# The products for keys, rotated queries and folded queries of a latent attention: two full-precision matmuls each, or five or six on rounded high and low parts

## The chip, the cores and the metric

The program runs on one core of a Trainium2 chip. The metric is the device time of one execution in microseconds; before the change it is the median of three executions. All values that enter and leave are float32.

## The reference, cut to what matters

Two transformer layers on 1024 tokens of 256 values. Only the first layer's attention is touched, and of it the part that makes rotated keys, rotated queries and folded queries:

```python
q_mid = rmsnorm(h @ q_a_w.T, q_a_ln_w)                 # 1024 x 192
q = (q_mid @ q_b_w.T)                                  # 16 heads of 128 + 64
q_nope, q_pe = q[..., :128], q[..., 128:]
kv_lora, k_pe = kv_a[..., :64], kv_a[..., 64:]         # kv_a = h @ kv_a_w.T, k_pe: 16 heads of 64
kv = rmsnorm(kv_lora, kv_a_ln_w) @ kv_b_w.T            # k_nope and v of each head
q_pe, k_pe = apply_rope(q_pe, cos, sin), apply_rope(k_pe, cos, sin)
scores = einsum(concat(q_nope, q_pe), concat(k_nope, k_pe)) * scale
probs = softmax(scores)
main_out = (probs @ v) @ o_w.T
# beside it a "pattern" attention with 16 heads of 16, then gates that mix the two,
# a mixture of experts, and a second layer
```

The kernel never forms `k_nope`: for each head `q_nope @ k_nope.T` is computed as (q_mid times a folded 192 x 64 matrix) times the 64 normalised values `kvT` that all heads share.

## The kernel before, in words

All orders are written out by hand: `pattern_order()`, `main_order()` and others list steps, and each of the five engines (TensorE, VectorE, ScalarE, GpSimd, and SP, which issues the DMAs) walks the same lists and executes its own part of each step; semaphores join them. Every engine's queue is in order.

The stages that matter here are these. Up to about 100 us the first layer's normalisation, the pattern attention's projections (`stgr`, through DRAM into `qstr`, `kstr`), the latents and the fold run. `act_latents` writes `qmTa` (q_mid transposed, values 0 to 127) and `qmTb` (values 128 to 191 in rows 0 to 63), and `act_fold` writes the folded matrices `waba` and `wabb`. From then to about 293 us comes the pattern attention: score matmuls (L1414), exponentials (L1435), value matmuls (L1457) and, running ahead, the maxima: max matmuls (L1281), reductions on VectorE (L1289), and the casts of the maxima (L1302, L1304), which the shift matmuls (L1314) need. From 306 to about 810 us comes the main attention in 32 units of 256 queries by 2 heads; four units are a pair of heads with all queries. A unit has four scores (L1712 to L1714, each on rounded high and low parts, on tiles `qk0h`, `qk0l`, `qk1h`, `qk1l`), a maximum on VectorE (L1721), exponentials (L1736), eight groups of four transposes (L1745) each with a copy (L1758 on ScalarE, L1763 on VectorE), one batch of value matmuls (L1805) and an output projection (L1826).

The products fill `qk0*` and `qk1*`. There are six for each pair p of heads, in the order of `FIRST`: R0 and R1 (rotated keys, two halves of the tokens), R2 (rotated queries, first half), Q0 and Q1 (folded queries), R3 (rotated queries, second half). Each is 128 x 512 and needs two matmuls over a contraction of 256 (keys) or 192 padded to 256 (queries), at L1536 in `pe_part`. Pair 0's six lie in the pattern attention, every eighth step, each cut in two around a max matmul (`pe_first`); pair p+1's lie in the first of pair p's units, one behind every fifth group of transposes (`PREP_EVERY`, `pe_prep`). Behind a product ScalarE copies the bank to `t12` (L1574); for a rotated one SP swaps its 32-row blocks with four DMAs (L1584), and GpSimd multiplies by cosines (L1596) and sines (L1598, which needs the swap), adds (L1601), and casts and subtracts into high and low parts (L1615, L1622); a folded one needs only the last two. `pe_score` waits, before the first score of each half pair, for the high and low parts that it reads. Three banks (4, 5, 7) turn round among transposes, projections and products, and each waits for its copy.

SP's queue holds, besides the swaps, the DMAs that write a unit's shares of the softmax to DRAM (`sp_shares`) and read them back spread over rows (`sp_spread`).

Of the kernel before, what the change touches and what calls it, by code (L numbers as in the profile page):

```python
# [334 lines left out]
def program(nc, a, out):  # L335
# [30 lines left out]
    x = sb("x", [128, NT, D], F32)  # L366
    hT = sb("hT", [128, 2, T], F32)
# [2762 lines left out]
```

## Time and profile before

| | |
|---|---|
| median of three executions | 1343.31 us (1342.86 to 1344.18) |
| profiled execution, its own time | 1348.52 us |
| its span, first to last instruction | 1346.6 us, mean granted TensorE clock 0.972 |
| busy share of TensorE, VectorE, ScalarE, GpSimd | 95%, 58%, 55%, 36% |
| line L1536 | 192 records of TensorE, 592 to 594 ns median as modelled |

A matmul's modelled duration overlaps the next one's, so what a matmul takes of the stream is read from start to start or from the chain, not from its own duration. A full-precision float32 matmul leaves two records (with one weight load each), a rounded one leaves one. An idle time in brackets stands ahead of the instruction, with what ended it.

### The profile page before, as it was taken

How to read it: one execution, taken by the hardware profiler on the slowest of the kernel's cores; microseconds unless marked ns; L12 is line 12 of the kernel's file. 1: busy time of each engine (PE TensorE's matmuls, PEld its weight loads, DVE VectorE, ACT ScalarE, POOL GpSimd, SP SyncE). 2: the span in 40 equal slices, each digit the busy share in tenths (PEclk: the TensorE clock that was granted, in tenths of full speed). 3: DMA queues.
4: the chain of work that ended last, by engine and by line, in shares of the span. 5: the costliest groups of instructions: out<-in, count | busy, mean ns of one | idle time of the engine just before them, and what ended most of it. 6: DMA issues, size and time to landing. Idle time of an engine off the chain costs nothing.

```text
span 1346.6 us, 22054 instructions
## 1 busy us (share of the span) xinstructions
PE 1278.6 (95%) x8233; PEld 873.7 (65%) x8233; DVE 776.1 (58%) x1221; ACT 734.5 (55%) x1364; POOL 487.3 (36%) x439
## 2 busy tenths in 40 slices
PE   7879999999999999999999999999978998889998
PEld 5633443357777777777777777788853444578997
DVE  4478987624545444444444566654767774575555
ACT  3438987775555555555555554333245667435553
POOL 5260045224656657474655303445200000331221
PEclk9969999999999999999999999999999999899999
DMA  8734000001010111111111203001331510101110
GB/s 330 192 75 82 1 10 17 9 1 29 20 33 17 31 25 24 25 24 24 24 24 25 63 13 138 24 25 47 72 81 39 114 36 1 32 15 32 49 40 32
DMA packets 54866, 63.90 MB, mean 47 GB/s; under 512 B 23997, under 2 KB 41149, under 8 KB 53693
## 3 DMA queue, kind: packets, MB, share of 16 engines
q1 hardware_dynamic: 54760, 62.50, 17.4%
q8 instruction: 66, 1.08, 0.4%
q14 instruction: 40, 0.32, 0.1%
HBM read 45.64 MB, written 8.45 MB: 40 GB/s over the span
## 4 chain that ended last, share of the span: by engine, by line
PE 82%; DVE 10%; ACT 3%; issue 2%; DMA 2%; SPq 0%; POOL 0%; ACTq 0%; DVEq 0%; POOLq 0%
PE bank L1805 9%; PE bank L1745 8%; PE bank L1457 7%; PE bank L1536 6%; PE bank L2002 5%; PE bank L2004 5%; PE bank L2003 5%; PE bank L1712 4%; PE bank L1714 4%; PE bank L1713 4%; PE bank L1414 4%; PE bank L1281 2%; PE bank L1826 2%; DVE mpc L1356 2%; PE bank L1394 2%
## 5 line engine op out<-in xcount | busy, mean ns | idle before, releaser
L1721 DVE TENSOR_REDUCE nmq<-bank 128x1 f32<-128x1024 f32 x128 | 156.5, 1223 | 163.8 <-PE bank L1714 163.7
L1435 ACT ACTIVATE Pb<-bank 128x512 f32<-128x512 f32 (+3 forms) x355 | 180.8, 573 | 36.6 <-PE bank L1414 14.1
L1758 ACT ACTIVATE Pt<-bank 128x512 f32<-128x512 f32 x187 | 110.6, 594 | 121.9 <-PE bank L1745 121.0
L1289 DVE TENSOR_REDUCE mp<-bank 128x2 f32<-128x1024 f32 x128 | 154.2, 1223 | 34.0 <-PE bank L1281 33.2
L1736 ACT ACTIVATE Pq<-bank,nmq 128x1024 f32<-128x1024 f32 x127 | 141.7, 1115 | 56.3 <-DVE nmq L1721 56.2
L1745 PE MATMUL bank<-idf,Pq 128*128 128x128 f32 x1016 | 145.8, 275 | 1.4 <-ACT Pq7l L1736 1.2
L1745 PEld LDWEIGHTS bank<-idf,Pq 128*128 128x128 f32 x1016 | 119.2, 140 | 39.3 <-issue 15.6
L1712 PE MATMUL bank<-qk1h,qk0h 128*128 128x512 f32 x256 | 120.6, 471 | 0.0
L1356 DVE TENSOR_REDUCE mpc<-bank 128x2 f32<-128x1024 f32 (+2 forms) x96 | 88.4, 954 | 47.5 <-PE bank L1344 25.2
L1805 PE MATMUL bank<-Pt,kvx 128*64 128x256 f32 x992 | 114.1, 382 | 0.0
L1457 PE MATMUL bank<-Pb,vx 128*17 128x256 f32 (+3 forms) x1222 | 108.9, 416 | 0.7 <-ACT OTa L1471 0.5
L1714 PE MATMUL bank<-qk1h,qk0l 128*128 128x512 f32 x256 | 101.2, 395 | 0.0
L1713 PE MATMUL bank<-qk1l,qk0h 128*128 128x512 f32 x256 | 100.4, 392 | 0.0
L1805 PEld LDWEIGHTS bank<-Pt,kvx 128*64 128x64 f32 x992 | 68.6, 137 | 40.5 <-issue 9.3
L1598 POOL TENSOR_TENSOR t<-t,sinT 128x512 f32<-128x512 f32 x32 | 41.0, 1280 | 107.0 <-DMA t<-t 107.0
L1977 POOL TENSOR_TENSOR cTt<-cTt,gab 128x256 f32<-128x256 f32 x8 | 6.1, 758 | 190.6 <-DVE cTt L1972 190.4
L1414 PE MATMUL bank<-qstr,kstr 64*128 64x512 f32 x256 | 72.1, 507 | 1.0 <-ACT Pb L1435 0.6
L2204 POOL TENSOR_TENSOR hl<-hf,hh 128x512 fp32r<-128x512 f32 x32 | 41.2, 1288 | 84.1 <-ACT hh L2191 84.1
L1596 POOL TENSOR_TENSOR Rt<-t,cosT 128x512 f32<-128x512 f32 x32 | 41.0, 1282 | 72.9 <-ACT t L1574 71.0
L2416 POOL TENSOR_TENSOR v1l<-wr,v1h 128x512 fp32r<-128x512 f32 x25 | 32.1, 1289 | 96.3 <-ACT v1h L2411 96.3
L1414 PEld LDWEIGHTS bank<-qstr,kstr 64*128 64x128 f32 x256 | 28.6, 188 | 58.2 <-ACT Pb L1435 36.4
L1816 DVE TENSOR_TENSOR OTm<-bank,Rs 128x256 f32<-128x256 f32 x32 | 13.6, 424 | 89.4 <-PE bank L1805 87.1
(344 smaller groups left out, 2948.5 us busy)
## 6 DMA issues: line engine op xcount, KB each, us to landing
t<-t SPq DMA_DIRECT2D x128, 64.0 KB
wr<-wf SPq DMA_DIRECT2D x25, 256.0 KB, 2.7
wraw<-wf SPq DMA_DIRECT2D x8, 768.0 KB, 4.3
scratch<-stgr SPq DMA_DIRECT2D x4, 1024.0 KB, 7.8
Rs<-shares SPq DMA_DIRECT2D x64, 64.0 KB, 3.8
scratch<-stg SPq DMA_DIRECT2D x8, 384.0 KB, 2.6
qst<-scratch SPq DMA_DIRECT2D x9, 256.0 KB, 8.6
owT<-owT SPq DMA_DIRECT2D x1, 2048.0 KB, 11.3
```

The costliest lines, as they stand in the source:

```text
L1289: e.tensor_reduce(mp[:, w % 3, :, j, kh], wide[slot][:], AX, ALU.max).then_inc(ring_ok, 1)
L1356: e.tensor_reduce(mpc[:, w // 2 % 3, a0:a0 + 2, j, kh], wide[slot][:, :, 0:c], AX, ALU.max).then_inc(ring_ok, 1)
L1414: e.matmul(bank[b][:], kst2[r, hp, kt * 128:kt * 128 + 128], qst2[r, hp, cols(half)], start=True, stop=True).then_inc(st_mm[0], 1)
L1435: e.activation(PBR[l][i % len(PBR[l])][:, 0:c], bank[b][:, 0:c], ACT.Exp, scale=0.25).then_inc(exp_ok[0], 1)
L1457: last = e.matmul(bank[6][32 * a:32 * a + 17, to:to + c], vx[:, t, h * 17:h * 17 + 17], PBR[l][i % len(PBR[l])][:, q0:q0 + c], start=(t == ...
L1712: e.matmul(o, qh[:, qs], kh[:, ks], start=True, stop=False)
L1713: e.matmul(o, qh[:, qs], kl[:, ks], start=False, stop=False)
L1714: last = e.matmul(o, ql[:, qs], kh[:, ks], start=False, stop=True)
L1721: e.tensor_reduce(nmq[:, n % 8:n % 8 + 1], scores(u, i), AX, ALU.max, negate=True).then_inc(mp_ok, 1)
L1736: e.activation(probabilities(u, i)[:], scores(u, i), ACT.Exp, bias=nmq[:, n % 8:n % 8 + 1], accum_out=sums[:, u % 2, i:i + 1]).then_inc(ex ...
L1745: last = e.transpose(bank[b][:, 128 * c:128 * c + 128], probabilities(u, 2 * (c % 2) + c // 2)[:, 128 * k:128 * k + 128], idf[:])
L1805: last = e.matmul(bank[6][64 * hd:64 * hd + 64, 0:256], kvx[:, k, :], transposed(u, k)[:, 256 * hd:256 * hd + 256], start=(k < 1), stop=(k ...
```

## The change

Operands of the six products are no longer read as float32. Each is split into a rounded part ("high", type fp32r) and the rounded remainder ("low"), and a product becomes the sum of high x high, low x high and high x low. Six rounded matmuls make a key product, five a query product.

- Moving operands, once, on GpSimd in `pool_rounded`, behind its pattern memsets and ahead of pair 0: `hT` gives `kmh` and `kml` (`kml` lies over `hT`), `qmTa` gives `qah` and `qal`. Of the 64 values in `qmTb` SP first makes a second copy in rows 64 to 127 (`sp_below`, two DMAs with the one for the folded matrices); `qbs` then holds the high part in rows 0 to 63 and the low part in rows 64 to 127, so that its stationary operand, with the weights in both halves of the rows, makes high x high and low x high in one matmul.
- Weights: `wkpe`, `wqpa`, `wqpb`, which were loaded whole, are loaded pair by pair, 128 KB each, into `wks` and `wqs`, and GpSimd splits them into `wkh`, `wkl`, `wqh`, `wql`; it splits the folded ones, `wab`, into `lth`, `ltl`. The load of the next keys' weights is issued behind R2's swap, that of the queries' behind R0's swap; the splits stand behind Q0 (keys), R3 (folded) and R0 (queries).
- GpSimd's two memsets at the start (`pool_rest`) go.

```diff
 
         cs = cols(ROPE[part[1]][1] if part[0] == "rope" else part[1])
         if part[0] == "rope" and ROPE[part[1]][0] == 1:
-            two = [(wkpe[:, k, p, :], hT[:, k, cs]) for k in range(2)]
-        elif part[0] == "rope":
-            two = [(wqpa[:, p, :], qmTa[:, cs]), (wqpb[:, p, :], qmTb[:, cs])]
+            if 0 in ks:
+                e.wait_ge(wt_ok, SPLIT2["k", p])
+                e.wait_ge(rounded, 12)
+            two = [[(wkh[:, k, :], kmh[:, k, cs]), (wkh[:, k, :], kml[:, k, cs]), (wkl[:, k, :], kmh[:, k, cs])] for k in range(2)]
         else:
-            two = [(w[:, 2 * p:2 * p + 2, :].rearrange("p h c -> p (h c)"), q[:, cs]) for w, q in ((waba, qmTa), (wabb, qmTb))]
+            if part[0] == "rope":
+                hi, lo = wqh, wql
+                if 0 in ks:
+                    e.wait_ge(wt_ok, SPLIT2["q", p])
+            else:
+                hi, lo = lth, ltl[:, :, p, :]
+                if 0 in ks:
+                    e.wait_ge(wt_ok, SPLIT2["lat", p])
+            if 0 in ks:
+                e.wait_ge(rounded, ROUNDED)
+            two = [[(hi[:, 0, :], qah[:, cs]), (hi[:, 0, :], qal[:, cs]), (lo[:, 0, :], qah[:, cs])],
+                   [(hi[:, 1, :], qbs[:, cs]), (lo[:, 1, :], qbs[:, cs])]]
         for k in ks:
-            last = e.matmul(o, *two[k], start=(k == 0), stop=(k == 1))
+            for n, (w, q) in enumerate(two[k]):
+                last = e.matmul(o, w, q, start=(k == 0 and n == 0), stop=(k == 1 and n == len(two[1]) - 1))
         if 1 in ks:
             last.then_inc(rp_mm if part[0] == "rope" else lt_mm, 1)
 
@@ -1543,11 +1578,6 @@
         b, free = BANK_P0[k]
         if not second:
             e.wait_ge(*free)
-            if k == 0:
-                e.wait_ge(d_w4, 48)
-                e.wait_ge(lat_ok, LAT_ALL)
-                e.wait_ge(fold_ok, 6)
-                e.wait_ge(rest_ok, 2)
         pe_part(e, 0, FIRST[k], bank[b][:], (1,) if second else (0,))
...
-    def pool_rest(e):
-
-        e.memset(qmTb[64:128, :], 0.0).then_inc(rest_ok, 1)
-        e.memset(wabb[64:128, :, :], 0.0).then_inc(rest_ok, 1)
-        e.wait_ge(rest_ok, 2)
+    def sp_below(e):
+
+        e.wait_ge(lat_ok, LAT_ALL)
+        e.dma_start(qmTb[64:128, :], qmTb[0:64, :]).then_inc(d_below, 16)
+        e.wait_ge(fold_ok, 6)
+        e.dma_start(wab[64:128, 1, :, :], wab[0:64, 1, :, :]).then_inc(d_below, 16)
+
+    def pool_rounded(e):
+
+        e.wait_ge(pj_mm, 8)
+        e.wait_ge(gate_mm, 4)
+        e.wait_ge(gate_v, 8)
+        for k, h in itertools.product(range(2), range(2)):
+            e.tensor_copy(kmh[:, k, cols(h)], hT[:, k, cols(h)]).then_inc(rounded, 1)
+        for k, q in itertools.product(range(2), range(4)):
+            ts = slice(256 * q, 256 * q + 256)
+            e.wait_ge(rounded, 2 * k + q // 2 + 1)
+            e.tensor_tensor(kml[:, k, ts], hT[:, k, ts], kmh[:, k, ts].bitcast(F32), ALU.subtract).then_inc(rounded, 1)
+        e.wait_ge(lat_ok, LAT_ALL)
+        for h in range(2):
+            e.tensor_copy(qah[:, cols(h)], qmTa[:, cols(h)]).then_inc(rounded, 1)
+        for q in range(4):
+            ts = slice(256 * q, 256 * q + 256)
+            e.wait_ge(rounded, 12 + q // 2 + 1)
+            e.tensor_tensor(qal[:, ts], qmTa[:, ts], qah[:, ts].bitcast(F32), ALU.subtract).then_inc(rounded, 1)
+        e.wait_ge(d_below, 32)
+        for h in range(2):
+            e.tensor_copy(qbh[:, cols(h)], qmTb[:, cols(h)]).then_inc(rounded, 1)
+        e.wait_ge(rounded, 20)
+        for q in range(4):
+            ts = slice(256 * q, 256 * q + 256)
+            e.tensor_tensor(qbs[64:128, ts], qmTb[64:128, ts], qbh[64:128, ts].bitcast(F32), ALU.subtract).then_inc(rounded, 1)
+        e.wait_ge(rounded, 24)
+        for h in range(2):
+            e.tensor_copy(qbs[0:64, cols(h)], qmTb[0:64, cols(h)]).then_inc(rounded, 1)
+        e.wait_ge(rounded, ROUNDED)
+
+    def sp_weights_k(e, p):
+
+        if p:
+            e.wait_ge(rp_mm, 4 * p - 2)
+        e.dma_start(wks[:], a["wkpe"][p]).then_inc(d_wk, 16)
+
+    def sp_weights_q(e, p):
+
+        if p:
+            e.wait_ge(rp_mm, 4 * p)
+        e.dma_start(wqs[:], a["wqpe"][p]).then_inc(d_wq, 16)
+
+    def pool_weights_k(e, p):
+        e.wait_ge(d_wk, 16 * (p + 1))
+        if p:
+            e.wait_ge(rp_mm, 4 * p - 2)
+        e.tensor_copy(wkh[:], wks[:]).then_inc(wt_hi, 1)
+        e.wait_ge(wt_hi, SPLIT2["k", p])
+        e.tensor_tensor(wkl[:], wks[:], wkh[:].bitcast(F32), ALU.subtract).then_inc(wt_ok, 1)
+        e.wait_ge(wt_ok, SPLIT2["k", p])
+
+    def pool_weights_q(e, p):
+        e.wait_ge(d_wq, 16 * (p + 1))
+        if p:
+            e.wait_ge(rp_mm, 4 * p)
+        e.tensor_copy(wqh[:], wqs[:]).then_inc(wt_hi, 1)
+        e.wait_ge(wt_hi, SPLIT2["q", p])
+        e.tensor_tensor(wql[:], wqs[:], wqh[:].bitcast(F32), ALU.subtract).then_inc(wt_ok, 1)
+        e.wait_ge(wt_ok, SPLIT2["q", p])
+
+    def pool_weights_l(e, p):
+        if p:
+            e.wait_ge(lt_mm, 2 * p)
+        else:
+            e.wait_ge(fold_ok, 6)
+            e.wait_ge(d_below, 32)
+        e.tensor_copy(lth[:], wab[:, :, 2 * p:2 * p + 2, :].rearrange("p a h c -> p a (h c)")).then_inc(wt_hi, 1)
+        e.wait_ge(wt_hi, SPLIT2["lat", p])
+        e.tensor_tensor(ltl[:, :, p, :], wab[:, :, 2 * p:2 * p + 2, :].rearrange("p a h c -> p a (h c)"), lth[:].bitcast(F32), ALU.subtract).then_inc(wt_ok, 1)
+        e.wait_ge(wt_ok, SPLIT2["lat", p])
...
         pool_stack2(e, slice(4, 8))
+        pool_rounded(e)
+        pool_weights_k(e, 0)
+        pool_weights_q(e, 0)
+        pool_weights_l(e, 0)
         for p in range(8):
             if p < 2:
                 pool_keys(e, p)
             for k in range(len(FIRST)):
                 pool_product(e, p, k)
+                if k == 0 and p:
+                    pool_weights_q(e, p)
+                elif k == 3 and p < 7:
+                    pool_weights_k(e, p + 1)
+                elif k == 5 and p < 7:
+                    pool_weights_l(e, p + 1)
         for s in MAIN:
...
-        for d, n in ((wkpe, "wkpe"), (wqpa, "wqpa"), (wqpb, "wqpb")):
-            e.dma_start(d[:], a[n]).then_inc(d_w4, 16)
+        sp_weights_k(e, 0)
+        sp_weights_q(e, 0)
         sp_scratch2(e, 2)
         sp_scratch2(e, 3)
         sp_stack2(e, 2)
         e.dma_start(cosT[:], a["cosT"]).then_inc(d_cs, 16)
         e.dma_start(sinT[:], a["sinT"]).then_inc(d_cs, 16)
+        sp_below(e)
         for k in range(len(FIRST)):
             sp_swap(e, 0, k)
+            if k == 2:
+                sp_weights_k(e, 1)
         for s in MAIN:
             if s[0] == "prep":
                 sp_swap(e, s[1], s[2])
+                if s[2] == 0:
+                    sp_weights_q(e, s[1])
+                elif s[2] == 2 and s[1] < 7:
+                    sp_weights_k(e, s[1] + 1)
```

In the host's layout `wkpe` and `wqpe` become pair-major, and `wqpe`'s second half repeats the 64 rows.

On TensorE, R2 of pair 1, behind four transposes in unit 1. The names are the moving operand and then the stationary one. Before:

```order
L1745 MATMUL bank<-idf,Pq_155 128x128
L1745 MATMUL bank<-idf,Pq_159 128x128
L1536 MATMUL bank<-qmTa,wqpa 128x512
L1536 MATMUL bank<-qmTb,wqpb 128x512
L1712 MATMUL bank<-qk1h_131,qk0h_129 128x512
```

and of the change:

```order
L1847 MATMUL bank<-idf,Pq_163 128x128
L1847 MATMUL bank<-idf,Pq_167 128x128
L1571 MATMUL bank<-qah,wqh 128x512
L1571 MATMUL bank<-qal,wqh 128x512
L1571 MATMUL bank<-qah,wql 128x512
L1571 MATMUL bank<-qbs,wqh 128x512
L1571 MATMUL bank<-qbs,wql 128x512
L1814 MATMUL bank<-qk1h_139,qk0h_137 128x512
```

Two matmuls became five at the same place, between the same transposes and the same score.

On GpSimd, the end of R0 of pair 1 and the start of R1. Before:

```order
L1615 CAST qk1h_136<-Rt 64x512
L1622 TENSOR_TENSOR qk1l_143<-Rt,qk1h_135 64x512
L1622 TENSOR_TENSOR qk1l_144<-Rt,qk1h_136 64x512
L1596 TENSOR_TENSOR Rt<-t_145,cosT 128x512
L1598 TENSOR_TENSOR t_145<-t_145,sinT 128x512
```

and of the change:

```order
L1645 CAST qk1h_144<-Rt 64x512
L1652 TENSOR_TENSOR qk1l_151<-Rt,qk1h_143 64x512
L1652 TENSOR_TENSOR qk1l_152<-Rt,qk1h_144 64x512
L1718 CAST wqh<-wqs 128x256
L1720 TENSOR_TENSOR wql<-wqs,wqh 128x256
L1626 TENSOR_TENSOR Rt<-t_153,cosT 128x512
L1628 TENSOR_TENSOR t_153<-t_153,sinT 128x512
```

The split of the query weights stands between the two products.

On SP, from the last table to the first DMA of unit 0's spread (20 swap DMAs are five products'). Before:

```order
L2951 DMA cosT<-cosT 128x1024
L2952 DMA sinT<-sinT 128x1024
L1584 DMA t_145<-t_145 32x512 x20
L1781 DMA shares<-rcp_60 128x4x1
L1792 DMA Rs<-shares 64x2x128 x2
```

and of the change:

```order
L3062 DMA cosT<-cosT 128x1024
L3063 DMA sinT<-sinT 128x1024
L1659 DMA qmTb<-qmTb 64x1024
L1661 DMA wab<-wab 64x1024
L1614 DMA t_153<-t_153 32x512 x12
L1697 DMA wks<-wkpe 128x256
L1614 DMA t_153<-t_153 32x512 x8
L1703 DMA wqs<-wqpe 128x256
L1883 DMA shares<-rcp_60 128x4x1
L1894 DMA Rs<-shares 64x2x128 x2
```

The two copies stand behind the tables, a load of key weights behind the third swap, and a load of query weights between a swap and the shares.

## Rows read from the trace of the kernel before

**Rows 1.** The page: busy us, share of the span, instructions.
```profile
PE 1278.6 (95%) x8233; PEld 873.7 (65%) x8233; DVE 776.1 (58%) x1221; ACT 734.5 (55%) x1364; POOL 487.3 (36%) x439
```

**Rows 2.** Busy time by windows: the first of the main stage's.
```profile
core 0: us, PE busy (x) PEld busy (x) DVE busy (x) ACT busy (x) POOL busy (x), PEclk, DMA share, GB/s
...
306.00:365.00 59.00, 59.00 (x344) 42.88 (x343) 28.89 (x37) 32.80 (x58) 32.59 (x31) 1.00 0.12 26
```

**Rows 3.** The chain that ended last, 320 to 420 us.
```profile
by line: PE bank L1745 22.7%; PE bank L1805 21.6%; PE bank L1536 15.6%; PE bank L1714 11.9%; PE bank L1712 11.6%; PE bank L1713 11.5%; PE bank L1826 5.2%
...
326.48 1.72 PE bank L1536 x4
```

**Rows 4.** The same chain, 730 to 860 us: start, length, what.
```profile
731.10 3.60 PE bank L1805 x32
...
748.28 3.60 PE bank L1805 x32
...
762.06 3.60 PE bank L1805 x32
```

**Rows 5.** Line L1536: ns min, median, max of its key matmuls.
```profile
L1536 PE MATMUL bank<-hT,wkpe x64: 592/592/697, 187.3 to 708.8; 128*128 128x512 f32 x64
```

**Rows 6.** Timeline of TensorE, 440 to 475 us: start, duration.
```profile
448.14 1.04 PE L1745 MATMUL bank<-idf,Pq 128*128 128x128 f32 x8
...
449.48 0.39 PE L1714 MATMUL bank<-qk1h,qk0l 128*128 128x512 f32 x1
449.71 0.39 PE L1712 MATMUL bank<-qk1h,qk0h 128*128 128x512 f32 x1
...
450.40 0.60 PE L1745 MATMUL bank<-idf,Pq 128*128 128x128 f32 x4
```

**Rows 7.** The chain that ended last, 184 to 306 us.
```profile
187.33 1.08 PE bank L1536 x2
...
188.84 1.05 PE bank L1536 x2
...
269.04 0.51 ACT Pb L1435
```

**Rows 8.** Timeline of GpSimd, 0 to 260 us.
```profile
33.44 1.59 POOL L1056 TENSOR_TENSOR raw<-raw,lnw 128x256 f32<-128x256 f32 x2 [2.79 <-ACT raw L1008]
...
186.27 2.13 POOL L1640 CAST qk1h<-kvT 64x1024 fp32r<-64x1024 f32 x2 [85.84 <-issue]
...
197.45 1.29 POOL L1615 CAST qk1h<-Rt 64x512 fp32r<-64x512 f32 x2
198.83 2.64 POOL L1622 TENSOR_TENSOR qk1l<-Rt,qk1h 64x512 fp32r<-64x512 f32 x2
```

**Rows 9.** DMA issues: KB each, median us from issue to landing.
```profile
cosT<-cosT SPq DMA_DIRECT2D x1, 512.0 KB, 17.4
```

**Rows 10.** Timeline of all engines, 96 to 113 us.
```profile
96.92 3.51 POOL L906 MEMSET kstr<- 16x4096 f32 x1
...
98.47 2.00 DVE L1302 CAST mc<-nm 128x8 fp32r<-128x8 f32 x1
...
112.52 0.17 DVE L1302 CAST mc<-nm 128x8 fp32r<-128x8 f32 x1
```

**Rows 11.** Timeline of all engines, 320 to 353 us, pair 1.
```profile
323.01 1.27 POOL L1596 TENSOR_TENSOR Rt<-t,cosT 128x512 f32<-128x512 f32 x1 [0.17 <-POOL qk1l L1622]
...
345.59 2.61 POOL L1622 TENSOR_TENSOR qk0l<-t,qk0h 64x512 fp32r<-64x512 f32 x2
...
350.97 0.48 PE L1712 MATMUL bank<-qk1h,qk0h 128*128 128x512 f32 x1
```

**Rows 12.** Timeline of all engines, 501 to 523 us, pair 4.
```profile
501.53 2.46 SPq L1584 DMA_DIRECT2D t<-t  x4
...
505.50 1.27 POOL L1598 TENSOR_TENSOR t<-t,sinT 128x512 f32<-128x512 f32 x1 [2.40 <-DMA t<-t]
...
509.64 2.63 POOL L1622 TENSOR_TENSOR qk1l<-Rt,qk1h 64x512 fp32r<-64x512 f32 x2
...
522.10 1.02 PE L1536 MATMUL bank<-qmTa,wqpa 128*128 128x512 f32 x2
```

More of the change, by code:

```diff
@@ L405, in program @@
     WKPE = A.at
-    wkpe = A.sb("wkpe", [128, 2, 8, 128], F32)
+    kmh = A.sb("kmh", [128, 2, T], F32R)
     WQP = A.at
-    wqpa = A.sb("wqpa", [128, 8, 128], F32)
-    wqpb = A.sb("wqpb", [128, 8, 128], F32)
+    qah = A.sb("qah", [128, T], F32R)
+    WQS = A.at
+    wqs = A.sb("wqs", [128, 2, 128], F32)
+    wqh = A.sb("wqh", [128, 2, 128], F32R)
+    wkh = A.sb("wkh", [128, 2, 128], F32R)
+    lth = A.sb("lth", [128, 2, 128], F32R)
     WAB = A.at
-    waba = A.sb("waba", [128, 16, 64], F32)
-    wabb = A.sb("wabb", [128, 16, 64], F32)
+    wab = A.sb("wab", [128, 2, 16, 64], F32)
     MO = A.at
@@ L427, in program @@
     gsb = A.sb("gsb", [128, 2], F32)
+    kml = sb("kml", [128, 2, T], F32R, at=HT)
+    qal = sb("qal", [128, T], F32R, at=QMT)
+    qbs = sb("qbs", [128, T], F32R, at=QMT + 4 * T)
+    qbh = sb("qbh", [128, T], F32R, at=WSP)
+    wql = sb("wql", [128, 2, 128], F32R, at=WQS)
+    ltl = sb("ltl", [128, 2, 8, 128], F32R, at=WAB)
     pctx = sb("pctx", [128, NT, D], F32, at=HTP)
@@ L980, in pool_vx_ones @@
         e.memset(vx[:].rearrange("p i (h c) -> p (i h) c", c=17)[:, :, 16:17], 1.0).then_inc(vx_one, 1)
-    d_w2, d_k, d_w3, d_w4, d_cs = sem("d_w2"), sem("d_k"), [sem("d_w30"), sem("d_w31")], sem("d_w4"), sem("d_cs")
+    d_w2, d_k, d_w3, d_cs = sem("d_w2"), sem("d_k"), [sem("d_w30"), sem("d_w31")], sem("d_cs")
     raw_mm, raw_ok, gw_ok = sem("raw_mm"), sem("raw_ok"), sem("gw_ok")
     rms_v, rms_s, gat_v, gat_s = sem("rms_v"), sem("rms_s"), sem("gat_v"), sem("gat_s")
-    qkv_ok, kvx_ok, lat_mm, lat_ok, lnw_ok = (sem(n) for n in (
-        "qkv_ok", "kvx_ok", "lat_mm", "lat_ok", "lnw_ok"))
+    qkv_ok, lat_mm, lat_ok, lnw_ok = (sem(n) for n in (
+        "qkv_ok", "lat_mm", "lat_ok", "lnw_ok"))
     LAT_ALL = 6
@@ L1087, in act_latents @@
         e.activation(kvT[:, cs], bank[6][:], ACT.Copy).then_inc(lat_ok, 1)
-    rest_ok = sem("rest_ok")
+    d_wk, d_wq, d_below = sem("d_wk"), sem("d_wq"), sem("d_below")
+    rounded, wt_hi, wt_ok = sem("rounded"), sem("wt_hi"), sem("wt_ok")
+    ROUNDED = 26
+    SPLITS = [("k", 0), ("q", 0), ("lat", 0)]
+    for p_ in range(1, 8):
+        SPLITS += [("k", p_), ("lat", p_), ("q", p_)]
+    SPLIT2 = {s_: n_ + 1 for n_, s_ in enumerate(SPLITS)}
     fold_mm, fold_ok, fold_v = sem("fold_mm"), sem("fold_ok"), sem("fold_v")
     def fold_rows(g):
-        return (128, waba, 8 * (g // 2), 0) if g % 2 == 0 else (64, wabb, 8 * (g // 2), 128)
+        return (128, wab[:, 0, :, :], 8 * (g // 2), 0) if g % 2 == 0 else (64, wab[:, 1, :, :], 8 * (g // 2), 128)
     def fold_bank(g):
@@ L3066, in layout @@
     kpe = kva[64:].reshape(8, 2, 64, 256)[:, ::-1].reshape(1024, 256).T
-    d["wkpe"] = np.ascontiguousarray(kpe.reshape(2, 128, 8, 128).transpose(1, 0, 2, 3))
+    d["wkpe"] = np.ascontiguousarray(kpe.reshape(2, 128, 8, 128).transpose(2, 1, 0, 3))
     qb = i["L0_attn_q_b_w"].reshape(16, 192, 192)
     qpe = qb[:, 128:, :].reshape(8, 2, 64, 192)[:, ::-1].reshape(8, 128, 192).transpose(2, 0, 1)
-    d["wqpa"], d["wqpb"] = np.ascontiguousarray(qpe[:128]), cat(qpe[128:], np.zeros_like(qpe[128:]))
+    d["wqpe"] = np.ascontiguousarray(np.stack([qpe[:128], cat(qpe[128:], qpe[128:])], 1).transpose(2, 0, 1, 3))
     d["qbn"] = np.ascontiguousarray(qb[:, :128, :].transpose(1, 0, 2))
```

6 lines of the change are left out of this document (4 added, 2 removed).

## The prediction

> **What bounds the kernel now.** I read the page first: TensorE is busy 95% of the span [rows 1], which alone says little, since ends of matmuls are modelled. So next the windows of 59 us over the stage where 42 of the 48 changed products run, units 0 to 27 of the main attention, from 306 us: in the first TensorE is busy for all 59 us at a granted clock of 1.00 (the 2.4 GHz level), VectorE, ScalarE and GpSimd for 29 to 33 [rows 2]; the seven behind it read alike. Then the chain that ended last, in 100 us of that stage: TensorE's lines make up all of it, with no wait for another engine and no issue time, and L1536, the changed line, is 15.6% [rows 3]. Last, a test of whether a shorter product shortens the stream: the same batch (L1805) starts 17.18 us apart where two products lie between and 13.78 apart where none does, so (17.18 - 13.78) / 2 = 1.70 us for one [rows 4]. The chain itself has 1.72 for a product [rows 3]. So without products the stream runs on with nothing else taking the room: a microsecond off L1536 is one off the span, until something else is late.
>
> **The products.** A product is two full-precision matmuls of 512 columns, each two records (64 records for the 32 key matmuls [rows 5]; the other 64 matmuls are the same shape). Four records are 1.72 us, 0.43 each. The change issues six rounded matmuls for a key product (two halves of the contraction, each high x high, low x high, high x low) and five for a rotated or folded query one (three and two, since the second half carries high and low parts in one operand). Their price stands in the score matmuls: the same shape on rounded operands, each with its own stationary operand as here. Transposes end at 448.14 + 0.87 = 449.01 (0.87 is two groups at the chain's 0.44), the next start at 450.40, six matmuls between: 1.39 / 6 = 0.232 us; start to start two rows have 0.23 [rows 6]. A key product becomes 6 x 0.232 = 1.39 and saves 0.33; another becomes 5 x 0.232 = 1.16 and saves 0.56. Seven pairs in the main stage: 7 x (2 x 0.33 + 4 x 0.56) = 20.3 us.
>
> A page speaks to this. The Trainium skill, "FP8 and Floating Point Precision", TensorE Precision Notes, says that true FP32 takes four passes through the array. Two such matmuls would be eight passes against six or five, 0.215 us a pass, and 27.5 us saved over 48 products, if all passes cost alike. The rows agree on 0.43 for a record of two passes but have 0.232 for a rounded matmul.
>
> **The first pair** has its six products in the pattern attention, each cut in two around two max matmuls, 1.08 + 1.05 us on the chain [rows 7]. The surplus of 0.4 over 1.72 I put down to the switches between full-array and 64-row matmuls, which stay; the rest changes as above, 2 x 0.33 + 4 x 0.56 = 2.9 us. Behind them the chain crosses an exponential of ScalarE here and there [rows 7], so 0 is the other end; I take 2.9, since most steps there are TensorE's. So far 23.2 us.
>
> **GpSimd's one-time rounding.** GpSimd is idle for 85.84 us up to 186.27. A cast of 512 columns takes 1.29 / 2 = 0.64, a subtraction of 512 takes 2.64 / 2 = 1.32, one of 256 half of that [rows 8]. Keys: four casts and eight quarters, 2.6 + 5.3; queries: six casts and eight quarters, 3.9 + 5.3; together 17 us, and under 4 for three weight splits. In between it waits for two transfers that copy rows 0 to 63 to rows 64 to 127, which stand behind the cosine tables on SP's queue; the tables took 17.4 us to land [rows 9], the copies would land near 118. Ready near 130, against the first product at 187.33: the idle time hides it, uncovered it would cost its 20 us.
>
> What it can cost there is VectorE's casts of the maxima (L1302). One that met a GpSimd memset took 2.00 us and ended as the memset did; the next, with GpSimd idle, took 0.17 [rows 10]. Two casts, near 112 and 123, now meet GpSimd instructions of 0.32 to 0.66 us. Bounds 0 and 1.3 us; I take 0.2, since only the rest of an instruction is waited for and one cast in two leads the chain at all. The Trainium skill, "GPSIMD Engine Reference", Specifications, says that GpSimd shares its SBUF interfaces with VectorE; the trace agrees with its 2.00 against 0.17.
>
> **Weight splits in the loop.** Three times a pair GpSimd gains a cast and a subtraction of 128x256: 0.32, and 0.66 to 0.80 (two multiplications of that shape take 1.59 [rows 8]), with hand-overs 1.1 to 1.3 us. That is 3.3 to 3.9 us in a pair of 4 x 13.78 + 6 x 1.70 = 65.3 us, of which GpSimd is busy 36 [rows 2]. Its queue is in order, so what stands behind a split matters:
> - The query split stands behind R0. In pair 1, R1 starts 0.17 us after R0's last subtraction, so there is no slack, and R1, R2 and Q0 shift by 1.1 to 1.3. Q0's low part, which the first score of unit 4 needs, ended at 345.59 + 2.61 = 348.20, and that score started at 350.97, 2.8 us in hand [rows 11]. By then TensorE is 2 x 0.33 + 3 x 0.56 = 2.3 us earlier: a stall of 0.6 to 0.8, I take 0.8.
> - In pair 4, R0's GpSimd work ends at 509.64 + 2.63 = 512.27, and R2, the next product with query weights, starts at 522.10 [rows 12]: 9.8 us for a split of 1.3.
> - The key and folded splits stand behind Q0 and R3. Products come five transposes apart, some 10 us, and a folded one takes GpSimd 1.28 + 2.64, a rotated one some 12: the lag of one is made good by the next.
> - TensorE's new waits before a product are for semaphores reached before; the score at 350.97 has seven waits and no idle time ahead of it [rows 11]. Nothing.
>
> **SP's queue** loses three transfers of 2 MB near 44 us and gains two of 128 KB there, the two copies, and 14 of 128 KB in the loop, behind R0's and R2's swap. One costs some 2.46 / 4 = 0.6 us of issue [rows 12]; it delays what is queued behind it, the shares and through them R1's swap. That wait lies beside the shift above: nothing more, 1 us a pair as the other end. The two memsets removed from GpSimd's start had nobody waiting: nothing.
>
> **Sum:** 23.2 - 0.2 - 0.8 = 22.2 us off. The profiled execution, 1348.52, becomes 1326.3; it is 5.2 us above the median of the three runs, so I forecast 1343.31 - 22.2 = **1321.1**.
>
> **Rivals.**
> - *Some is swallowed* (0.12): the first pair's 2.9 go to ScalarE behind them, and the loop gives another microsecond back. 22.2 - 3.9 = 18.3, 1325. For: the exponential in the chain. Against: it is one of few.
> - *GpSimd, the swaps and ScalarE's copies fall behind in every pair* (0.17). For: R1 goes back to back behind R0 in pair 1, and a pair gets 3 us shorter while GpSimd's work grows by 3.9. Against: GpSimd is idle for 29 us of each pair, mostly in waits for later things. At 1 to 2 us in each of seven pairs, 7 to 14 back: 1328 to 1335.
> - *A rounded matmul costs a pass, 0.215* (0.04): 256 x 0.017 = 4.3 more off, 1316.8; so by the page above. Against: 0.23 in every score.
> - *Slower* (0.03). The query weights land late: their transfer is issued behind R0's swap, near 504, and R2 starts at 522.10 - 0.7. With a split of 1.3 the transfer may take 16 us; R0's swap landed 1.5 us after its last issue, by GpSimd's start at 505.50 [rows 12], but the cosine tables took 17.4. Each microsecond above 16 stalls TensorE, with every transpose and score behind it, in seven pairs; from 16 + 22.2 / 7 = 19.2 us it decides for slower, and 21 us gives 1343.3 + 7 x 1.8 = 1356.
> - *It does not do what it says* (0.02): rounded matmuls on these operands run as two records of 0.43. 256 x 0.86 = 220 against 48 x 1.72 = 83 us: 1480.
>
> **Numbers.** The forecast case, 1319 to 1324, has 0.62. The range 1317 to 1330 takes in the pass-pace case, the swallowed one and the cheap end of falling behind, and leaves some 0.17 out. 0.2% is 2.7 us, about what a measurement of this kernel can tell from no change: faster 0.93, same 0.02 (the dearest end of falling behind), slower 0.05.
>
> **What would show it.** Right: 256 single records on the product line, 0.23 apart; L1805's batches some 16.1 us apart with two products between and 13.78 with none; a chain of TensorE alone in the loop, but for a stall under 1 us before unit 4's first score; GpSimd's rounding over before 135 us. Wrong: TensorE waiting for low parts or weight splits in several pairs; ScalarE's copy of a product held by a swap with scores waiting behind it; VectorE casts of over a microsecond near 112 us; rounded products at another pace.

## The result, and the profile after

The changed kernel takes 1323.84 us, median of four executions (1316.35 to 1326.55), against 1343.74 for the kernel before beside it (1342.86 to 1344.27): a ratio of 0.9846, 95% interval 0.9824 to 0.9869, so 17.6 to 23.7 us off. In a later session five executions have a median of 1321.97, ratio 0.9853 (0.9829 to 0.9877). The profiled execution took 1326.55 us, its span 1324.6.

The page of the changed kernel: busy time, and the granted clock of TensorE in 40 slices of 33 us.

```profile
PE 1253.9 (95%) x8297; PEld 884.3 (67%) x8297; DVE 775.9 (59%) x1221; ACT 732.5 (55%) x1364; POOL 530.4 (40%) x511
...
PEclk9979999999999999999999999999979999899999
```

Beside [rows 1], TensorE's busy time is 25 us less and its share the same 95%: the share told nothing before and tells nothing now. GpSimd has 43 us more; VectorE and ScalarE have what they had, within 2 us. Where the time went is seen in the chain that ended last. The changed kernel, two stretches of it (start, length, what):

```profile
503.30 1.39 PE bank L1571 x6
...
512.81 0.59 PE bank L1847 x4
513.40 1.16 PE bank L1571 x5
...
712.19 3.60 PE bank L1907 x32
...
728.25 3.60 PE bank L1907 x32
741.99 3.60 PE bank L1907 x32
755.74 3.60 PE bank L1907 x32
```

L1571 is the product line, L1907 the batch of value matmuls. A key product is six records in 1.39 us, another five in 1.16, where four records took 1.72 [rows 3]. The batches stand 728.25 - 712.19 = 16.06 us apart with two products between them, and 13.75 with none; before it was 17.18 and 13.78 [rows 4].

What the whole change gave to the stage it is in is read between two marks: the start of the first product, and the start of the last addition of the main attention's output into x, on VectorE. First and last start stand in the rows of one line (count, ns min/median/max, then the starts). The kernel before, then the changed one in a second trace of it:

```profile
L1536 PE MATMUL bank<-hT,wkpe x64: 592/592/697, 187.3 to 708.8; 128*128 128x512 f32 x64
L1840 DVE TENSOR_TENSOR x<-x,bank x32: 677/689/691, 330.9 to 818.6; 128x512 f32<-128x512 f32 x32
```

```profile
L1571 PE MATMUL bank<-kmh,wkh x32: 389/474/500, 185.0 to 685.9; 128*128 128x512 f32 x32
L1942 DVE TENSOR_TENSOR x<-x,bank x32: 675/687/692, 324.9 to 793.8; 128x512 f32<-128x512 f32 x32
```

818.6 - 187.3 = 631.3 us before and 793.8 - 185.0 = 608.8 after: 22.5 less. I call this time "the stage" below, and "the loop" the units of the main attention in it. The first trace of the changed kernel has 613.0: it lost 4.2 us in one place, which the section on the prediction takes up.

### The profile page after: what moved, and what is told of

It is laid out like the page before. It is cut to its first block, busy times and chain, and to the rows that moved or that the text cites. A ratio compares the mean times of both kernels' runs of the same rounds, so it can differ in the third digit from the quotient of the medians.

```text
span 1324.6 us, 22340 instructions
## 1 busy us (share of the span) xinstructions
PE 1253.9 (95%) x8297; PEld 884.3 (67%) x8297; DVE 775.9 (59%) x1221; ACT 732.5 (55%) x1364; POOL 530.4 (40%) x511
## 4 chain that ended last, share of the span: by engine, by line
PE 77%; DVE 11%; DMA 4%; ACT 3%; issue 3%; SPq 2%; POOL 1%; ACTq 0%; DVEq 0%; POOLq 0%
PE bank L1907 8%; PE bank L1847 8%; PE bank L1479 7%; PE bank L2104 6%; PE bank L2105 6%; PE bank L2106 6%; PE bank L1571 4%; PE bank L1814 4%; PE bank L1436 4%; PE bank L1816 4%; PE bank L1815 4%; DVE mp L1311 2%; PE bank L1303 2%; PE bank L1928 2%; DVE mpc L1378 2%
## 5 line engine op out<-in xcount | busy, mean ns | idle before, releaser
L1838 ACT ACTIVATE Pq<-bank,nmq 128x1024 f32<-128x1024 f32 x127 | 141.6, 1115 | 52.2 <-DVE nmq L1823 52.1
L1907 PE MATMUL bank<-Pt,kvx 128*64 128x256 f32 x992 | 114.1, 382 | 0.0
L1814 PE MATMUL bank<-qk1h,qk0h 128*128 128x512 f32 x256 | 109.8, 429 | 0.0
L1816 PE MATMUL bank<-qk1h,qk0l 128*128 128x512 f32 x256 | 101.3, 396 | 0.0
L1907 PEld LDWEIGHTS bank<-Pt,kvx 128*64 128x64 f32 x992 | 68.6, 137 | 37.7 <-issue 6.6
L1628 POOL TENSOR_TENSOR t<-t,sinT 128x512 f32<-128x512 f32 x32 | 41.0, 1281 | 99.7 <-DMA t<-t 99.7
L1303 PE MATMUL bank<-kstr,qstr 64*128 64x512 f32 x256 | 59.9, 445 | 3.7 <-DVE mp L1311 3.6
```

The lines of the kernel that those rows point to most:

```text
L1814: e.matmul(o, qh[:, qs], kh[:, ks], start=True, stop=False)
L1816: last = e.matmul(o, ql[:, qs], kh[:, ks], start=False, stop=True)
L1838: e.activation(probabilities(u, i)[:], scores(u, i), ACT.Exp, bias=nmq[:, n % 8:n % 8 + 1], accum_out=sums[:, u % 2, i:i + 1]).then_inc(ex ...
L1907: last = e.matmul(bank[6][64 * hd:64 * hd + 64, 0:256], kvx[:, k, :], transposed(u, k)[:, 256 * hd:256 * hd + 256], start=(k < 1), stop=(k ...
```

## The experiments

Every kernel was traced. The table has, from the trace, the start of the first product, the stage, what lies behind it up to the end of the span, and TensorE's idle time from 304 to 366 us, the first of seven windows of 62 us (62 less its busy time). In the other six windows TensorE is busy for all 62 us in every kernel, but for 428 to 490 in the first trace. The ratio is to the executions of the kernel before in the same session.

| kernel | median us (executions) | ratio, 95% | first product | stage | behind | idle |
|---|---|---|---|---|---|---|
| before, two traces | 1343.74 (4), 1343.21 (1) | | 187.3, 184.1 | 631.3, 631.3 | 528.0, 525.9 | 0, 0 |
| changed, first trace | 1323.84 (4) | 0.9824 to 0.9869 | 185.6 | 613.0 | 526.0 | 0.59 |
| the same, second | 1321.97 (5) | 0.9829 to 0.9877 | 185.0 | 608.8 | 526.2 | 0.44 |
| the same, third | 1324.35 (1) | | 184.9 | 608.7 | 528.8 | 0.64 |
| no loads in the loop | 1320.81 (6) | 0.9815 to 0.9867 | 186.0 | 608.4 | 521.3 | 0.26 |
| no work on weights in the loop | 1323.40 (6) | 0.9830 to 0.9880 | 187.3 | 609.7 | 528.9 | 1.62 |
| longer splits | 1326.88 (4) | 0.9834 to 0.9898 | 185.5 | 609.8 | 530.5 | 1.70 |
| no swaps | 1325.27 (4) | 0.9821 to 0.9906 | 185.9 | 608.4 | 523.5 | 0 |
| swap in two DMAs | 1326.08 (4) | 0.9827 to 0.9900 | 188.3 | 613.3 | 524.3 | 3.58 |
| keys in fp32 | 1326.20 (6) | 0.9838 to 0.9896 | 186.2 | 614.1 | 526.0 | 0.88 |
| high parts only | 1292.55 (4) | 0.9590 to 0.9649 | 186.7 | 577.3 | 529.0 | 1.90 |
| the same, no low weights made | 1292.02 (4) | 0.9584 to 0.9662 | 185.8 | 575.4 | 527.2 | 2.33 |

Read the columns against each other. Ahead of the first product and behind the stage, where these kernels differ little or not at all, one trace and the next differ by up to 4 and 9 us, whatever the kernel; unedited kernels give 631.3 twice, and 608.8 and 608.7. So the stage shows 0.5 us where a median shows 3, unless a transfer is late as in the first trace (613.0).

**The changed kernel again, unedited.**

> The changed kernel once more, unedited, for its spread (1316.35 to 1326.55 us in four runs, where the kernel before has 1342.86 to 1344.27). Theory A (the weights' loads and splits inside the loop make GpSimd and the swaps late, now in one pair, now in another, and TensorE then stands and loses its clock): again a spread of some 10 us, median 1321 to 1325, and the profile shows one or two stops of 1 to 3 us in the loop at a rotation's swap or a low part. Theory B (the stop in pair 3 of the first profile was a single late landing that any run may have): median nearer 1318, and no stop in most pairs; the spread would then be there in the next two kernels too.

Neither theory's case as written. The median, 1321.97, is theory A's, but the one stop in the stage, at pair 1's products, is of 0.44 us where A wanted 1 to 3, and the spread was 1321.4 to 1325.55 and not 10 us; pair 3 has no stop, as theory B had it. And the premise fell: the kernel before, in the same session, went from 1338.76 to 1349.78 in eleven executions. The spread is in both kernels.

**No loads of weights in the loop.**

```diff
-            if k == 2:
-                sp_weights_k(e, 1)
...
-                if s[2] == 0:
-                    sp_weights_q(e, s[1])
-                elif s[2] == 2 and s[1] < 7:
-                    sp_weights_k(e, s[1] + 1)
```

> Leaves out the key and query weights' loads of pairs 1 to 7 (14 DMAs of 128 KB on SyncE's queue); the splits stay, each reading what the last one left. Theory A, in the form that the loads hold up the swaps behind them: 3 to 6 us under the unedited kernel of the same call (about 1318), spread under 2 us, no swap landing over 7 us. In the form that GpSimd's splits do it: same as unedited, within 1 us. Theory B (late landings are chance): same median within 1 us, spread of some 10 us stays.

On GpSimd (not shown) each split of pairs 1 to 7 reads what the last one left, so its work stays. The stage is 608.4 against 608.8 and 608.7, the spread still 9 us (1317.64 to 1326.97). The 14 loads cost at most 0.4 us altogether.

**No work on weights in the loop.**

```diff
-                if k == 0 and p:
-                    pool_weights_q(e, p)
-                elif k == 3 and p < 7:
-                    pool_weights_k(e, p + 1)
-                elif k == 5 and p < 7:
-                    pool_weights_l(e, p + 1)
...
-                e.wait_ge(wt_ok, SPLIT2["k", p])
+                e.wait_ge(wt_ok, SPLIT2["k", 0])
```

> Leaves out all work on weights inside the loop: the loads of pairs 1 to 7 and the splits of the key, query and folded weights; every pair multiplies with pair 0's rounded weights. TensorE does the same matmuls. Theory A: 1316 to 1318, spread under 2 us, the copy of Q1 in pair 1 no longer waits for the low parts of Q0. Theory B: the median falls by the 1.3 us of pair 1's wait at most, and the spread stays.

The stage is 609.7, no shorter than unedited, and the median 1323.40 where theory A wanted 1316 to 1318. ScalarE's copies of products to `t12` in pair 1, in the kernel without any work on weights (start, duration, idle time before it and its releaser):

```profile
336.06 0.60 ACT L1604 ACTIVATE t<-bank 128x512 f32<-128x512 f32 x1 [4.07 <-DMA t<-t]
...
346.91 0.60 ACT L1604 ACTIVATE t<-bank 128x512 f32<-128x512 f32 x1 [3.13 <-POOL qk0l L1652]
```

The second is Q1's copy, which waits for Q0's low part because both go through `t12`. It waits 3.13 us with the splits gone; unedited, it waits 1.96:

```profile
340.71 2.65 POOL L1652 TENSOR_TENSOR qk0l<-t,qk0h 64x512 fp32r<-64x512 f32 x2
...
343.45 0.60 ACT L1604 ACTIVATE t<-bank 128x512 f32<-128x512 f32 x1 [1.96 <-POOL qk0l L1652]
...
344.10 0.66 PE L1847 MATMUL bank<-idf,Pq 128*128 128x128 f32 x4 [0.44 <-ACT t L1604]
```

By itself this doesn't clear the splits, since R2's swap was slower in this execution. What does is the chain that ended last, traced back from the stop. Unedited:

```profile
309.10 8.17 DMA shares<-rcp
...
317.29 0.66 SPq L1894
...
318.71 0.56 SPq L1614
...
320.58 2.19 DMA t<-t
...
322.83 1.30 POOL t L1628
...
325.62 0.51 SPq L1614
...
327.44 5.00 DMA t<-t
...
332.51 1.29 POOL t L1628
```

A unit's shares go to DRAM (8.17 us). The DMAs that read them back (L1894) wait for that in SP's queue, and R1's swap (the first L1614) is issued behind them. R1's multiplication by the sines (L1628), R2's swap, R2's sines, Q0's low part and Q1's copy follow. No split of weights is in this chain, and no work on R0. It is the same chain without work on weights, with R2's swap slow in the issue itself:

```profile
327.80 3.48 SPq L1614
...
331.32 2.61 SPq L1614
...
333.97 1.98 DMA t<-t
...
336.02 1.29 POOL t L1628
```

Counted from the first product, in all traces whose TensorE does the same matmuls and whose swaps in pair 1 are complete and not late:

| kernel | R1's sines start | R2's sines start | idle |
|---|---|---|---|
| changed, three traces | 137.7, 137.8, 138.0 | 147.7, 147.5, 147.6 | 0.59, 0.44, 0.64 |
| no loads | 136.8 | 147.3 | 0.26 |
| no work on weights | 137.2 | 148.7 | 1.62 |
| longer splits (next run) | 137.7 | 148.8 | 1.70 |

The idle time is the start of R2's sines less 147.1, within 0.15 us in all six. That start is set by R2's swap, which took 6.9 to 7.7 us from its first issue to there in the first four traces, 8.8 without work on weights and 7.9 with longer splits; why it varies no run shows. R1's sines come 0.5 to 1.2 us earlier only where the loads are gone, which fits the load's issue ahead of the shares in SP's queue. So the 1.62 us is the slower swap and no price of this edit, and the splits are not what makes Q0's low part late.

That low part ends at 340.71 + 2.65 = 343.36 unedited. From the last addition behind the pattern attention (301.4, and 306.2 before) that is 142.0 us, and the 348.20 of before [rows 11] is 142.0 too (142.1 and 142.2 in the other traces of the changed kernel, 141.6 in the other of before). It hardly moved, while TensorE comes to Q1 2.3 us earlier (two key products and three others). Before, Q1's copy started at 348.55, 0.35 us behind that low part:

```profile
348.55 0.60 ACT L1574 ACTIVATE t<-bank 128x512 f32<-128x512 f32 x1 [0.51 <-PE bank L1536]
```

2.3 less 0.35 is close to the 1.96 us that ScalarE now waits, and TensorE, with transposes behind that copy, stands for the last 0.44 of it.

**Longer splits.** Each cast of weights is made four times.

```diff
-        e.tensor_copy(wqh[:], wqs[:]).then_inc(wt_hi, 1)
-        e.wait_ge(wt_hi, SPLIT2["q", p])
+        for n in range(4):
+            e.tensor_copy(wqh[:], wqs[:]).then_inc(wt_hi, 1)
+            e.wait_ge(wt_hi, 4 * SPLIT2["q", p] - 3 + n)
```

> Each split of weights has its cast four times in place of once, some 1.4 us more GpSimd work for each of three splits a pair, so the split takes 2.6 us and GpSimd is busy 45 of 62 us. Theory A (steady pairs have room, pair 1 alone is late): pairs 2 to 7 stay at 62.3 us and TensorE without idle time; pair 1 loses 1.4 us more for the query split ahead of Q0, 610 to 611.5 us from the first product to the last addition into x. Rival (GpSimd's lag passes from pair to pair, as the forecast's third case had it): each pair loses 1 to 4 us, 617 or more.

The stage is 609.8, 1.0 to 1.1 more than unedited, all of it in the first window (idle 1.70 against 0.44 to 0.64); six windows are full, with GpSimd busy 45 of 62 us in five of them. That looks like theory A's pair 1, but the table above says otherwise: R1's sines start where they did, and R1's sum at most 0.3 us later (139.45 us from the first product against 139.1 to 139.4). The rest is R2's swap, slower by 0.7 to 1.0 us. So a split longer by 1.4 us is free in six pairs of seven and costs at most 0.3 us in pair 1.

**No swaps.** GpSimd multiplies the unswapped copy by the sines, and ScalarE's next copy waits for that multiplication in place of the swap (not shown).

```diff
-        for q in range(4):
-            e.dma_start(t12[32 * (q ^ 1):32 * (q ^ 1) + 32, 1, :], t12[32 * q:32 * q + 32, 0, :]).then_inc(d_sw, 16)
...
-            e.wait_ge(d_sw, 64 * (r + 1))
-            e.tensor_tensor(t12[:, 1, :], t12[:, 1, :], sinT[:, cs], ALU.mult).then_inc(rp_sin, 1)
+            e.tensor_tensor(t12[:, 1, :], t12[:, 0, :], sinT[:, cs], ALU.mult).then_inc(rp_sin, 1)
```

> Leaves out the four DMAs of each rotation's swap (GpSimd multiplies the unswapped copy by sinT); all of GpSimd's instructions, the weights' loads and splits and TensorE's stay. Theory C (the one stop left in the loop, in pair 1, comes from TensorE now reaching pair 1's products some 4 us earlier while each product on GpSimd still waits 2 to 4 us for its swap; the weights have nothing to do with it, since without them the wait for Q0's low part was 3.1 us against 2.0): no idle time of TensorE between 304 and 366 us, 608.2 to 608.6 us from the first product to the last addition into x, and no wait of ScalarE's copies for GpSimd. Rival (GpSimd's own work in pair 1, rounding and splits, is the hold): the wait for the low part of Q0 stays at 1 us or more, idle time over 0.3 us.

Windows of the changed kernel unedited, of the one without work on weights and of the one without swaps, 304 to 366 us (length, then busy us of TensorE, its weight loads, VectorE, ScalarE, GpSimd; granted clock, DMA share, GB/s):

```profile
304.00:366.00 62.00, 61.56 (x391) 48.54 (x391) 32.28 (x43) 37.80 (x67) 41.49 (x43) 1.00 0.15 33
```

```profile
304.00:366.00 62.00, 60.38 (x379) 47.92 (x378) 30.43 (x41) 34.92 (x62) 36.51 (x35) 1.00 0.13 27
```

```profile
304.00:366.00 62.00, 62.00 (x391) 49.18 (x391) 33.06 (x43) 37.43 (x66) 42.92 (x44) 1.00 0.09 16
```

With 42.92 us of GpSimd's work and no swap there is no idle time; with 36.51 us of work and the swaps there is the most of the three. Theory C stands: the hold is in the swaps. The run takes away both parts of that hold at once, the transfers and R1's place behind the shares in SP's queue, so it doesn't say which counts for how much. The stage is 608.4.

**Swap in two DMAs.**

```diff
-        for q in range(4):
-            e.dma_start(t12[32 * (q ^ 1):32 * (q ^ 1) + 32, 1, :], t12[32 * q:32 * q + 32, 0, :]).then_inc(d_sw, 16)
+        for q in range(2):
+            e.dma_start(t12[64 * (q ^ 1):64 * (q ^ 1) + 64, 1, :], t12[64 * q:64 * q + 64, 0, :]).then_inc(d_sw, 16)
```

> Moves the same bytes of each swap in two DMAs of 64 partitions in place of four of 32 (halves of 64 rows change places, where the rotation wants halves of 32 within each head). SyncE issues for 1.2 us in place of 2.46. Theory C: the landing comes about 1.2 us earlier, GpSimd's waits for swaps fall by about a third (84.1 us in the loop of the unedited run), and pair 1's idle time of TensorE goes to 0.0 to 0.2 us; the time from the first product to the last addition into x is 608.3 to 608.8. Rival: the landing is set by the transfer itself and stays, and so does the stop.

Theory C's case did not come. SyncE issues a swap in 1.18 us, but GpSimd's waits for swaps add up to 84.7 us in 26 waits against 84.1 in 28, and without the one late swap in pair 1 (9.30, below) to 75.4 in 25: 3.0 us each, as unedited. So nothing was won by shorter issue, as the rival has it. The stage is 613.3 for the late swap.

**The keys' part undone.** GpSimd's rounding of `hT` and the splits of the keys' weights are gone too.

```diff
-            two = [[(wkh[:, k, :], kmh[:, k, cs]), (wkh[:, k, :], kml[:, k, cs]), (wkl[:, k, :], kmh[:, k, cs])] for k in range(2)]
+            two = [[(wks[:, k, :], hT[:, k, cs])] for k in range(2)]
```

> Undoes the keys' part of the change: the rotated keys' products are two fp32 matmuls again (hT by wks, unsplit), GpSimd's rounding of hT and its splits of the key weights are gone; queries and folded queries stay as changed. Theory A (TensorE bounds the loop and each product is worth what its pace gives): each key product 1.86 to 1.71 us in place of 1.39, 0.33 to 0.47 more, sixteen of them, so from the first product to the last addition into x 5 to 7 us longer than the 608.8 of the unedited run, about 614.5. Rival (the products wait anyway for swaps and GpSimd, so part of a longer product is free): under 3 us longer.

The stage is 614.1 against 608.8, 5.3 us more. That it is 16 x 0.33 to the tenth is in part luck: from the end of the first pair on (302.8 to 800.3) it is 5.1 more, 14 x 0.33 = 4.6 and 0.44 of longer idle time in pair 1, and the first pair gave back 0.2 of its 0.7. Where every product waits for nothing the price holds: the chain has 1.72 us for a key product and 1.16 or 1.17 for most of the others.

**High parts only.** This one leaves out the products with low parts, so its products are those of rounded operands alone.

```diff
-            two = [[(wkh[:, k, :], kmh[:, k, cs]), (wkh[:, k, :], kml[:, k, cs]), (wkl[:, k, :], kmh[:, k, cs])] for k in range(2)]
+            two = [[(wkh[:, k, :], kmh[:, k, cs])] for k in range(2)]
...
-            two = [[(hi[:, 0, :], qah[:, cs]), (hi[:, 0, :], qal[:, cs]), (lo[:, 0, :], qah[:, cs])],
-                   [(hi[:, 1, :], qbs[:, cs]), (lo[:, 1, :], qbs[:, cs])]]
+            two = [[(hi[:, 0, :], qah[:, cs])], [(hi[:, 1, :], qbs[:, cs])]]
```

> Leaves out the products with low parts: two rounded matmuls of 128x512 for each product in place of six and five, everything else as changed. By the pace of 0.232 us a pair loses 2*4*0.232+4*3*0.232 = 4.6 us and the kernel 7*4.6 = 32.5 in the loop and up to 4.6 in pair 0, if TensorE stays the bound: about 37 us under the unedited kernel, 1286. The rival is that GpSimd, the swaps and ScalarE's copies, already late in pairs 1 and 3, become the bound once TensorE's pair is 57.7 us long: then less than 28 us, and waits for low parts in every pair.

29.4 us under the unedited kernel by the medians and 31.5 by the stage, between the two expectations. From the end of the first pair on (the last addition behind the pattern attention, 301.8 and 301.4 us, to the last of the main one) it is 462.2 against 492.4, 30.2 less where 32.5 were expected, and 1.5 of the 2.3 missing are pair 1's wait, 1.90 against 0.44. All other windows are full: TensorE is the bound even at some 58 us a pair. The first pair gave 1.3 of 4.6 (115.1 us against 116.4); in that trace the clock was 0.97 between 190 and 304 us, where the next one has 1.00.

**The same, without making the low weights.**

```diff
-        e.tensor_copy(wqh[:], wqs[:]).then_inc(wt_hi, 1)
-        e.wait_ge(wt_hi, SPLIT2["q", p])
-        e.tensor_tensor(wql[:], wqs[:], wqh[:].bitcast(F32), ALU.subtract).then_inc(wt_ok, 1)
+        e.tensor_copy(wqh[:], wqs[:]).then_inc(wt_ok, 1)
```

> As the kernel with high parts only (the products with low parts left out), and the weights' low parts aren't made either: GpSimd loses three subtractions of 0.73 us a pair. Theory A: TensorE's pair stays 57.7 us and only pair 1's wait shrinks, by up to 1 us: 576 to 577.5 us from the first product to the last addition into x, where the kernel with high parts only has 577.3. Rival (GpSimd bound the loop there): 570 to 573.

The stage is 575.4, but the main part is 462.8, as before the edit (462.2), and pair 1's wait grew to 2.33. The 2 us are the first pair's, 112.6 against 115.1, at the full clock. So neither expectation was met: work taken from GpSimd gave nothing in the loop, not even in pair 1, as the swaps of theory C would have it.

**The kernel before and the changed one, once more.**

> The kernel before, unedited, for a second trace of it. Both theories: 631.3 us from the first product to the last addition into x within 0.5 us, as in its first trace; what the two traces of it differ by lies ahead of the first product and behind the loop, in stretches at the lower clock, up to 3 us in each.

> The changed kernel unedited, for a third trace of it: whether the late landing of one swap in pair 3 of the first trace (11.5 us) comes back. If it is chance: no swap landing over 8 us, loop 608.4 to 610 us from the first product to the last addition into x. If the change brings it: a wait of over 8 us for a swap again.

Both came out as expected: 631.3 to the tenth, with its first product 3.2 us earlier than in the first trace; and 608.7, longest wait for a swap 6.0 us.

## Why the prediction was right, step by step

The forecast was 1321.1 us with 1317 to 1330 as its range; measured were 1323.84 and 1321.97.

- **What bounds the kernel, and the price of a product.** Right to the hundredth: 1.39 and 1.16 us. With the keys undone the main part of the stage gave back 4.6 + 0.44 us, the forecast's term for fourteen key products and a longer wait in pair 1. The rival of one pass a matmul, 0.215, falls: 1.16 / 5 = 0.232.
- **The sum of the main stage, 20.3 us.** From the last addition behind the pattern attention to the last of the main one: 818.6 - 306.2 = 512.4 before, 793.8 - 301.4 = 492.4 after. That is 20.0, and 20.4 without the 0.44 us idle in it.
- **The first pair, 2.9 us.** 118.9 us before and 116.4 after: 2.5 us came, so 0.4 at most was swallowed. The chain has 0.92 + 0.89 us for a cut key product and 0.92 + 0.66 for another, 0.42 above the uncut price in both, so the surplus stayed as forecast; that it comes from switching between the shapes no run tests.
- **GpSimd's rounding.** Hidden. It was over at 125.4 us, 60 us ahead of the first product. VectorE's cast near 111 us took 0.17 us, but GpSimd was idle then, for 6.36 us up to 116.35, so that one tests nothing. The cast and subtraction near 122, beside GpSimd's work, took 0.55 together: 0.2 us more than the 0.34 with GpSimd idle (0.1 more in the second trace). The term taken was 0.2. Timelines of GpSimd and VectorE in the changed kernel:

```profile
116.35 1.17 POOL L1683 CAST qbh<-qmTb 128x512 fp32r<-128x512 f32 x2 [6.36 <-DMA wab<-wab]
...
124.70 0.73 POOL L1731 TENSOR_TENSOR ltl<-wab,lth 128x256 fp32r<-128x256 f32 x1
```

```profile
121.53 0.17 DVE L1324 CAST mc<-nm 128x8 fp32r<-128x8 f32 x1
121.74 0.38 DVE L1326 TENSOR_TENSOR mc<-nm,mc 128x8 fp32r<-128x8 f32 x1
```

- **Weight splits in the loop.** The duration was right (0.40 + 0.73 with a hand-over, 1.2 us). The stall, 0.8 forecast and 0.4 to 0.6 measured, was right in size by luck: its place and cause were not as forecast. The step that failed is the sentence that R1, R2 and Q0 shift by the length of the split, since R1 starts 0.17 us after R0. R1's sines waited another 2.99 us for the swap before, and that wait takes the split in:

```profile
327.28 1.28 POOL L1598 TENSOR_TENSOR t<-t,sinT 128x512 f32<-128x512 f32 x1 [2.99 <-DMA t<-t]
```

Q0's low part moved by 0 to 0.6 us over the traces and not by 1.1 to 1.3, counted from the last addition behind the pattern attention. And the place to look at was not unit 4's first score, with 2.8 us in hand, but Q1's copy with 0.35. What remains true is that TensorE got 2.3 us ahead of a chain that doesn't get shorter with it.
- **SP's queue.** Right in size: 0.4 us at most for all loads, by the run without them. But its path, over the shares to R1's swap, does not lie beside the splits' shift: it is the one that the chain takes.
- **What the sum says nothing of.** 22.5 us came in the stage, 19.9 and 20.7 in the medians. The rest is in what differs from execution to execution: ahead of the stage and behind it in every kernel, and in the first trace the 4.2 us of a late swap. Whether executions without a trace had such a swap is not known.

**The stop in pair 3** of the first trace is the one thing that the forecast's case had no room for; a copy of ScalarE held by a swap with scores behind it was one of its signs of being wrong. The chain through it (the DMA is the last of the four of R1's swap, from its issue on; L1814 to L1816 are scores):

```profile
441.02 11.48 DMA t<-t
...
452.61 0.60 ACT t L1604
...
453.26 1.12 PE bank L1847 x4
454.37 0.43 PE bank L1814
454.80 0.43 PE bank L1815
455.23 0.43 PE bank L1816
```

and TensorE's timeline there:

```profile
453.26 1.12 PE L1847 MATMUL bank<-idf,Pq 128*128 128x128 f32 x4 [2.41 <-ACT t L1604]
```

The swap landed 11.48 us after the last issue; elsewhere in the same chain it is 2.06 and 5.35. It held R2's copy on ScalarE, behind which exponentials and copies wait, so TensorE stood for 2.41 us. After that its 512-column matmuls went at 0.43 us each, the 1.2 GHz level (granted clock 0.50), for some 3.5 us: 4.2 us lost in all. In the trace of the kernel with two DMAs a swap in pair 1 had the same (GpSimd waited 9.30 us, TensorE's weight loads 4.0, the stage lost 4.5). These are two of ten traces of changed kernels with swaps, some 28 swaps each in the loop (a third long wait, 8.7 us in the kernel with keys in fp32, cost nothing). In the two traces of before the longest wait for a swap was 5.7 us. Whether the change makes such landings likelier is open: two in 280 against none in 56 can't tell.

## What to carry to other kernels

Where the chain is one engine's alone, price a replacement instruction by the same shape in the same trace, start to start: the sum of the main stage then came true to 1% here (20.4 against 20.3), and to 3% with the low parts left out (31.7 against 32.5, waits taken out). When the bound engine gets faster, look next for the chain of hand-overs beside it that does not get shorter, a buffer that product, swap and next copy share; relieving an engine in that chain gave nothing here, since what it waited for was a DMA. Count such a wait before adding an instruction's length to what stands behind it. And measure such a change between two marks around its stage: here that told 0.4 us, where medians of four to eleven executions moved by 3.

## What the runs showed of the hardware

- Four SBUF to SBUF DMAs of 64 KB, once issued, landed 2.06 us after the last one's issue at the quick end, after 5.35 and 5.00 in the same place of two traces, and once after 11.48. The Trainium skill, "DMA: Bandwidth & Descriptors", Latency and other measured facts, puts a DMA's fixed cost at about 2 us; the quick landings agree, the others are far above it, so a wait of this kind needs its slack counted from the longest one seen. In the late one hardly anything was moved: the DMA engines' busy tenths of the changed kernel from 425 to 470 us, 40 slices of 1.1 us, are empty from 444 to 456 us, while the landing is at 452.50.

```profile
DMA  0024440000000956200000000000443300040000
```

- TensorE stood still for 2.41 us and had the lower clock for some 3.5 us afterwards; that stop cost 4.2 us. After 3.58 us (the kernel with two DMAs) it had the lower clock for some 3.4 us. After waits of 0.44, 1.62, 1.90 and 2.33 us in pair 1 of other traces the granted clock stayed at 1.00.
- Two unedited kernels differed from trace to trace by 3 us ahead of the first product and, with those that differ only in the loop, by up to 9 us behind the stage, with granted clocks of 0.967 to 0.981 over the span.
